# Scores from 64-wide queries and keys in TensorE's row halves, softmax on two batches at once

## What is computed

```python
q = jnp.einsum('bsd,hde->bhse', x, Wq)
k = jnp.einsum('bsd,hde->bhse', x, Wk)
v = jnp.einsum('bsd,hdf->bhsf', x, Wv)
s_a = jnp.einsum('bhie,bhje->bhij', k, q) / e
attn = jax.nn.softmax(s_a, axis=-1)
ax = jnp.einsum('bhtf,bhit->bhfi', v, attn)
...
out = a_flat @ Wlt
```

## Time and profile before

| | us |
|---|---|
| median of 3 runs | 1500.25 |
| lowest, highest | 1497.04, 1500.66 |
| the profiled execution | 1500.72 |
| its span, first to last instruction | 1498.9 |
| TensorE matmul busy | 1399.7 (93%) |
| VectorE busy | 1184.3 (79%) |
| ScalarE busy | 1008.2 (67%) |
| GpSimd (POOL) busy | 788.0 (53%) |
| mean granted TensorE clock | 0.979 |

### The profile page before, as it was taken

One profiled execution on the slowest core, in us unless ns is written; L12 is line 12 of the kernel. 1 busy time (PEld: TensorE's weight loads), 2 busy tenths in 40 slices (PEclk: granted clock), 3 DMA queues, 4 the chain that ended last, 5 costly groups with the idle time before them and its releaser, 6 DMA issues.

```text
span 1498.9 us, 32061 instructions
## 1 busy us (share of the span) xinstructions
PE 1399.7 (93%) x7812; PEld 1121.1 (75%) x7812; DVE 1184.3 (79%) x3231; ACT 1008.2 (67%) x2311; POOL 788.0 (53%) x888
## 2 busy tenths in 40 slices
PE   5899999999999999999998988898987999999993
PEld 4677888888888888888886766666765888888871
DVE  2988898989899898989897688777777766666655
ACT  2677887878887888878786666666654555555540
POOL 1675444444444444444442477767666565665561
PEclk8999999999999999999999999999999999999997
DMA  3422222222222222222224988777755787777779
GB/s 85 154 76 73 88 100 76 91 80 87 87 80 91 76 91 80 101 80 91 79 78 144 297 273 273 219 233 227 223 172 198 279 292 254 249 251 246 243 284 362
DMA packets 180725, 245.76 MB, mean 164 GB/s; under 512 B 32641, under 2 KB 143761, under 8 KB 180657
## 3 DMA queue, kind: packets, MB, share of 16 engines
q1 hardware_dynamic: 159872, 206.57, 41.5%
q0 software_dynamic: 13920, 31.33, 6.4%
q10 hardware_dynamic: 6864, 7.09, 1.4%
HBM read 99.85 MB, written 89.51 MB: 126 GB/s over the span
## 4 chain that ended last, share of the span: by engine, by line
PE 70%; DVE 11%; POOL 7%; issue 7%; DMA 2%; ACT 2%; SPq 1%; DVEq 0%; POOLq 0%; ACTq 0%
PE bank L403 15%; PE bank L405 13%; PE bank L404 13%; PE pair_ps L1690 10%; PE bank L1621 5%; PE bank L1715 5%; POOL sorted_scratch L839 5%; PE pair_ps L1854 1%; PE bank L1611 1%; POOL rstdB L833 1%; PE bank L1789 1%; DMA yearly<-y_scratch 1%; PE pair_ps L405 1%; PE pair_ps L403 1%; PE bank L1629 1%
## 5 line engine op out<-in xcount | busy, mean ns | idle before, releaser
L697 POOL TENSOR_TENSOR prob<-expo,inv 92x368 f32<-92x368 f32 x256 | 205.0, 801 | 394.6 <-DVE inv L1219 394.6
L874 POOL DMA_INDIRECT y_scratch<-ytok,tin x198 | 194.0, 980 | 124.1 <-issue 91.9
L839 POOL DMA_INDIRECT sorted_scratch<-trow,posi x184 | 180.2, 979 | 96.0 <-issue 57.5
L1690 PE MATMUL pair_ps<-z,xnT 128*92 128x368 f32 x512 | 201.3, 475 | 0.0
L1212 DVE TENSOR_REDUCE peak<-pair_ps 92x4 f32<-92x368 f32 x256 | 136.1, 532 | 73.2 <-PE pair_ps L1690 73.1
L1403 DVE SCALAR_TENSOR_TENSOR hid_l<-bank,hid_h 128x512 fp32r<-128x512 f32 (+1 forms) x159 | 103.5, 655 | 93.7 <-ACT hid_h L1040 92.7
L914 ACT ACTIVATE z<-bank 128x368 f32<-128x368 f32 x254 | 121.2, 477 | 63.0 <-PE bank L405 55.9
L953 ACT ACTIVATE w2s<-bank 128x368 fp32r<-128x368 f32 x256 | 122.5, 478 | 47.4 <-PE bank L405 43.0
L960 ACT ACTIVATE expo<-cent 92x368 f32<-92x368 f32 x256 | 130.4, 509 | 31.2 <-DVE cent L1224 28.2
L1040 ACT ACTIVATE hid_h<-bank 128x512 fp32r<-128x512 f32 (+1 forms) x159 | 90.5, 569 | 78.9 <-PE bank L405 78.3
L1239 DVE TENSOR_TENSOR w2s<-bank,w2s 128x368 fp32r<-128x368 f32 x256 | 136.2, 532 | 6.0 <-ACT w2s L953 3.1
(11 more groups left out here) (274 smaller groups left out, 3875.3 us busy)
## 6 DMA issues: line engine op xcount, KB each, us to landing
ax_scratch<-val SPq DMA_DIRECT2D x64, 736.0 KB, 3.8
arow<-ax_scratch SPq DMA_DIRECT2D x92, 512.0 KB
w1t<-w1s SPq DMA_DIRECT2D x53, 512.0 KB, 3.2
w2t<-w2s SPq DMA_DIRECT2D x53, 512.0 KB, 3.0
tin<-sorted_scratch SPq DMA_DIRECT2D x46, 260.0 KB
xin<-in_x_dram SPq DMA_DIRECT2D x32, 372.0 KB
ywide<-y_scratch SPq DMA_DIRECT2D x32, 256.0 KB, 7.2
h_scratch<-hP SPq DMA_DIRECT2D x32, 184.0 KB, 5.1
```

The lines of the kernel that those rows point to most:

```text
L697: nc.gpsimd.tensor_tensor(prob[:, k % 2], expo[:, k % 2], inv[:, k % 2].unsqueeze(2).to_broadcast([S, HH, S]), ALU.mult).then_inc(prob_kep ...
L839: pool.indirect_dma_start(out=sorted_dram, out_offset=bass.IndirectOffsetOnAxis(ap=posi[:, q, choice, r:r + 1], axis=0), in_=trow[:, q, ch ...
L874: pool.indirect_dma_start(out=y_dram, out_offset=bass.IndirectOffsetOnAxis(ap=tin[:, b, r, D:D + 1].bitcast(I32), axis=0), in_=ytok[:, b % ...
L1690: mm(score_ps[k % 2][0:S, 0:GT], xnT[:, q, b * S:(b + 1) * S], z[:, b, half * HH:(half + 1) * HH, :], start=True, stop=True).then_inc(scor ...
```

## The change

The products of `Wq` and `Wk` are no longer formed. The opening splits the weights themselves (`split_qk`) into `wqk_h` and `wqk_l`, eight slots of 128 columns: slot 2t holds the queries' weights of heads 2t and 2t + 1 side by side, slot 2t + 1 those of the keys. `project_qk` takes the place of `make_z`, with the same three matmuls, places and steps, and `qk[:, s]` of z: rows 0 to 63 of a slot belong to the even head, rows 64 to 127 to the odd one. The scores of two units (two batches, four heads) are made together at the head of every even step: eight float32 matmuls of 92 columns of weights, 64 rows and 92 columns, which go to rows 0 to 63 and 64 to 127 by turns, the lower rows to the one score bank and the upper ones to the other. `peak`, `cent`, exp, `total` and `inv` each treat both units in one instruction: `peak`, `cent` and exp in the even step, `total` and `inv` in the odd one. POOL's product, the transposes, the mix and the values stay per unit. `cent` and `expo` keep their size and are now one room for a pair of units instead of two rooms by turns. Heads within four are now in the order 0, 2, 1, 3 (`head_of`), which the value weights and the place in `val` follow. The copy `xnT` is gone.

```diff
+def head_of(n):
+    return n // HH * HH + n % 2 * 2 + n % HH // 2
...
+        score_ps = pair_ps[0:S].rearrange("i (u n) -> i u n", u=2)[:, :, 0:GT].rearrange("i u (k t j) -> i u k t j", k=2, t=2)
...
-        Z_FIRST = {6: 9, 7: 11}
-        Z_MID = {2: 5, 3: 7, 5: 8}
-        Z_THEN = {1: 4, 2: 6, 6: 10}
+        QK_FIRST = {6: 9, 7: 11}
+        QK_MID = {2: 5, 3: 7, 5: 8}
+        QK_THEN = {1: 4, 2: 6, 6: 10}
...
-                at_least(pool, inv_kept, n + 1)
-                at_least(pool, exp_kept, n + 1)
+                at_least(pool, inv_kept, UN // 2 * g + k // 2 + 1)
+                at_least(pool, exp_kept, UN // 2 * g + k // 2 + 1)
...
-                A(z[:, :, h, :], room[:, 0:GT].rearrange("d (b j) -> d b j", b=GB), ACT.Copy).then_inc(z_kept, 1)
+                A(qk[:, h], room[:, 0:GT], ACT.Copy).then_inc(qk_kept, 1)
...
-                if exists(g):
-                    n = UN * g + k
-                    at_least(act, cent_kept, n + 1)
-                    at_least(act, prob_kept, n - 1)
-                    A(expo[:, k % 2], cent[:, k % 2], ACT.Exp, scale=1.0 / E).then_inc(exp_kept, 1)
+                if exists(g) and k % 2 == 0:
+                    pair = UN // 2 * g + k // 2
+                    at_least(act, cent_kept, pair + 1)
+                    at_least(act, prob_kept, 2 * pair)
+                    A(expo[:], cent[:], ACT.Exp, scale=1.0 / E).then_inc(exp_kept, 1)
...
+            def split_qk(j):
+                src = raw[:, j * H * E:(j + 1) * H * E].rearrange("d (t n) -> d t n", n=2 * E)
+                dve.wait_ge(ws_qk, 32)
+                V.tensor_copy(wqk_h[:, j:H:2], src).then_inc(wqkh_kept, 1)
+                dve.wait_ge(wqkh_kept, j + 1)
+                V.tensor_tensor(wqk_l[:, j:H:2], src, wqk_h[:, j:H:2].bitcast(F32), ALU.subtract).then_inc(wqkl_kept, 1)
...
+                pair = UN // 2 * g + k // 2
+                if exists(g) and k % 2 == 0:
+                    if k == 2 and exists(g + 1):
+                        at_least(dve, sixes_kept, g + 2)
+                    at_least(dve, score_done, 2 * (pair + 1))
+                    V.tensor_reduce(peak[:], score_ps, AX_X, ALU.max).then_inc(peak_kept, 1)
                 if k == 2 and exists(g + 1):
                     keep_moments(g + 1)
+                if exists(g) and k % 2 == 0:
+                    at_least(dve, peak_kept, pair + 1)
+                    at_least(dve, exp_kept, pair)
+                    V.tensor_tensor(cent[:].rearrange("i k (u t) j -> i u k t j", u=2), score_ps,
+                                    peak[:].unsqueeze(4).to_broadcast([S, 2, 2, 2, S]), ALU.subtract).then_inc(cent_kept, 1)
+                if exists(g) and k % 2 == 1:
+                    at_least(dve, exp_kept, pair + 1)
+                    V.tensor_reduce(total[:], expo[:], AX_X, ALU.add).then_inc(total_kept, 1)
+                    at_least(dve, total_kept, pair + 1)
+                    at_least(dve, prob_kept, 2 * pair)
+                    V.reciprocal(inv[:], total[:]).then_inc(inv_kept, 1)
...
-                    at_least(pe, z_kept, H * g + (half + 1) * HH)
-                    at_least(pe, cent_kept, n - 1)
-                    mm(score_ps[k % 2][0:S, 0:GT], xnT[:, q, b * S:(b + 1) * S], z[:, b, half * HH:(half + 1) * HH, :],
-                       start=True, stop=True).then_inc(score_done, 1)
+                if exists(g) and k % 2 == 0:
+                    half = k // GB
+                    at_least(pe, qk_kept, H * g + (half + 1) * HH)
+                    at_least(pe, cent_kept, UN // 2 * g + k // 2)
+                    for n in range(4):
+                        nk, t = n // 2, n % 2
+                        at = slice((k + nk) % GB * S, ((k + nk) % GB + 1) * S)
+                        for u in (0, 1):
+                            queries, keys = (qk[u * E:(u + 1) * E, half * HH + 2 * t + side, at] for side in (0, 1))
+                            ins = mm(score_ps[:, u, nk, t], keys, queries, start=True, stop=True)
+                            if n == 3:
+                                ins.then_inc(score_done, 1)
```

More of the change, by code:

```diff
@@ L34 @@
 WARM = 4
-LAG_S, LAG_T, LAG_TK, LAG_M, LAG_V = 1, 2, 3, 4, 8
+LAG_T, LAG_TK, LAG_M, LAG_V = 2, 3, 4, 8
 CT = 512
@@ L203, in build @@
         tokb = sb("tokb", [D, 1], stack=first)
-        pair_h = sb("pair_h", [D, H, D], F32R, stack=first)
-        pair_l = sb("pair_l", [D, H, D], F32R, stack=first)
+        wqk_h = sb("wqk_h", [D, H, 2 * E], F32R, stack=first)
+        wqk_l = sb("wqk_l", [D, H, 2 * E], F32R, stack=first)
         wv_h = sb("wv_h", [D, H, D], F32R, stack=first)
@@ L217, in build @@
         xtok = sb("xtok", [S, GB, D], stack=first)
-        xnT = sb("xnT", [D, 2, GT], stack=first)
         xn_h = sb("xn_h", [D, GT], F32R, stack=first)
@@ L222, in build @@
         xtok_l = sb("xtok_l", [S, 2, GB, D], F32R, stack=first)
-        z = sb("z", [D, GB, H, S], stack=first)
-        peak = sb("peak", [S, 2, HH], stack=first)
+        qk = sb("qk", [2 * E, H, GT], stack=first)
+        peak = sb("peak", [S, 2, 2, 2], stack=first)
         cent = sb("cent", [S, 2, HH, S], stack=first)
@@ L341, in build @@
         cs = sem("cs")
-        qkT_done, qkT_kept, pair_done, pair_kept = (sem(n) for n in ("qkT_done", "qkT_kept", "pair_done", "pair_kept"))
+        wqkh_kept, wqkl_kept = (sem(n) for n in ("wqkh_kept", "wqkl_kept"))
         split_v, split_lt, high_kept, low_kept, split_c = (sem(n) for n in (
@@ L968, in step @@
                         at_least(act, val_out[half], 16 * gv)
-                    A(val[:, half, :, h % HH, :], val_ps[:, 0:GT].rearrange("f (b i) -> f b i", b=GB),
+                    A(val[:, half, :, head_of(h) % HH, :], val_ps[:, 0:GT].rearrange("f (b i) -> f b i", b=GB),
                       ACT.Copy).then_inc(val_kept, 1)
-                keep_zs(g, k, Z_THEN)
+                keep_qks(g, k, QK_THEN)
                 if k == 0 and exists(g + 1):
@@ L1636, in turn_xn, with project_qk @@
                 ins.then_inc(xn_done, 1)
-            def make_z(g, h, room=front_ps[1], opening=False):
+            def project_qk(g, h, room=front_ps[1], opening=False):
                 if not opening:
-                    at_least(pe, z_kept, H * g + h)
+                    at_least(pe, qk_kept, H * g + h)
                 if h == 0:
-                    at_least(pe, xnT_kept, g + 1)
+                    at_least(pe, xnh_kept, g + 1)
                     at_least(pe, xnl_kept, g + 1)
@@ L1645, in make_z, with project_qks @@
                         at_least(pe, xT_kept, KC * (g + 2))
-                three(room[:, 0:GT], pair_h[:, h], pair_l[:, h], xn_h[:], xn_l[:],
-                      True, True).then_inc(z_done, 1)
-            def make_zs(g, k, when):
+                three(room[:, 0:GT], wqk_h[:, h], wqk_l[:, h], xn_h[:], xn_l[:],
+                      True, True).then_inc(qk_done, 1)
+            def project_qks(g, k, when):
                 if k in when and exists(g + when[k] // H):
-                    make_z(g + when[k] // H, when[k] % H)
+                    project_qk(g + when[k] // H, when[k] % H)
             for c in range(KC):
@@ L1657, in _ @@
                 embed(0, piece)
-            pe.wait_ge(ws_qk, 32)
-            for j in range(4):
-                for m in range(4):
-                    o = (4 * j + m) * E
-                    ins = nc.tensor.transpose(bank[2 + j][0:E, m * D:(m + 1) * D], raw[:, o:o + E], ident[:])
-                ins.then_inc(qkT_done, 1)
-            turn_first(0)
-            pe.wait_ge(qkT_kept, 4)
-            for j in range(2):
-                for m in range(4):
-                    h = 4 * j + m
-                    qT = raw[0:E, 2048 + h * D:2048 + (h + 1) * D]
-                    kT = raw[0:E, 2048 + (H + h) * D:2048 + (H + h + 1) * D]
-                    ins = mm(bank[6 + j][:, m * D:(m + 1) * D], qT, kT, start=True, stop=True)
-                ins.then_inc(pair_done, 1)
+            turn_first(0)
             for c in range(KC):
```

92 lines of the change are left out of this document (26 added, 66 removed).

## The result

| | before | after |
|---|---|---|
| median, us | 1499.78 (4 runs) | 1565.71 (4 runs) |
| lowest, highest | 1497.04, 1500.66 | 1563.86, 1566.89 |
| profiled execution (span) | 1500.72 (1498.9) | 1565.93 (1564.0) |
| TensorE matmul busy | 1399.7 (93%) | 1403.5 (90%) |
| VectorE busy | 1184.3 (79%) | 1150.8 (74%) |

The ratio is 1.044, 95% interval 1.0424 to 1.046: slower by 66 us. The forecast was 1597 with a range from 1535 to 1660.

What follows compares the result with a forecast made beforehand. TensorE was taken as the bound. Per group, 19.27 us of other work + 3.5 of new waits + 4 x 1.15 for bursts = 27.4, against 24.23; 32 groups add 101 us, the opening -4: 1597 us, range 1535 to 1660.

Steps and rivals of the forecast that it cites:

- the sign: TensorE's busy share in 150 to 750 us was to fall below 93%, with idle time in odd steps.
- The new waits: TensorE waits in odd steps for VectorE and ScalarE behind the pair softmax: 3.5 us per group, 112 us in all.
- step 2: Steps 2 to 3 of a group: with moments and varA in the chain, TensorE was to wait 1.19 us.
- X: Price of one score burst on TensorE, four per group: 1.15 us taken, against 1.24 for two scores before.
- overlap with both changes of form: Burst price if the row halves run together and entering and leaving the 64-row form is paid: 1.02 us.
- the gap at 22.0 us: About 0.2 us between matmul starts after the opening's 64-row matmuls, where 0.12 is usual; 0.15 booked per change of form.
- the high end: Burst price if the halves do not overlap and both changes of form are paid: 1.58 us.
- The opening: Start of the kernel: without four copies, pair products and their splits in the chain, 4 us less.
- the first rival: Halves gain fully, waits as forecast: X 0.72 to 1.02, 25.7 to 26.9 us per group, 1542 to 1581 us; chance 0.20.
- Halves one after the other: Row halves in the burst do not run side by side: X 1.28 to 1.58, 1614 to 1652 us; chance 0.15.
- The costly alternation: Each alternation of halves in a burst costs like a change of form: X about 2.5, near 1770 us; chance 0.03.
- The hidden chain: Longer VectorE and ScalarE chain before the odd step stays hidden, no new waits: 1427 to 1465 us; chance 0.12.

Runs made afterwards that it cites:

- E9: Changed kernel with the pair burst kept, but maximum, centring, exp, sum and reciprocal per unit with the old lags: 1507.45 us, 1.0044 of the kernel before.
- E2: Kernel before with its full-height scores, both units' scores at the head of the even step and the softmax on two units at once: 1620.19 us, 1.0797.
- E11: E9 with probability transposes first in odd steps, and moments and varA of step 2 behind mix_l: 1472.19 us, 0.981 of the kernel before.
- E1: Changed kernel with all four matmuls of the lower rows first, then those of the upper rows: 1614.67 us, 1.076 of the kernel before.
- E3: Changed kernel with row halves kept, but scores of one unit in every step and the softmax of the kernel before: 1498.31 us, 0.9986.
- E6: Changed kernel, even steps: VectorE makes probT_l and mix_l between maximum and centring, ScalarE does exp last: 1571.74 us, 1.0475 of the kernel before.
- E10: E7 with ScalarE's exp also last in the even step: 1564.61 us, 1.0424 of the kernel before.
- E5: Changed kernel with ScalarE's exp last in even steps, behind the value and qk copies: 1562.82 us, 1.0416 of the kernel before.
- E7: Changed kernel with the burst issued in the odd step before, behind the probability transposes and ahead of the values: 1534.62 us, 1.0228 of the kernel before.
- E12: Changed kernel, pair softmax kept, with the same two moves as E11: 1529.09 us, 1.0188 of the kernel before.

## Why the prediction was right

**What bounds.** Right. TensorE's own work was the whole chain before, and the trace had no room for a later VectorE. From 150 to 750 us TensorE's busy share is 552.44 of 600, 92.1%, under the 93% that the prediction named as the sign.

**The new waits.** Right in mechanism, place and releaser. Forecast from burst to odd step were 2.95, 3.55, 2.95 and 3.65 us; measured 2.94, 3.15, 2.95 and 3.61. The pieces that gave them: `peak` 921 ns and `cent` 912 (taken as 940), exp 817 (880).

Only step 2 was off, by 0.4, and that is `varA`. The prediction took the 2.79 us of before from maximum to TensorE and made it longer. In that stretch `varA` began while POOL's product of the probabilities ran, and ended with it:

```profile
411.26 0.80 POOL L697 TENSOR_TENSOR prob<-expo,inv 92x368 f32<-92x368 f32 x1 [1.75 <-DVE inv L1219]
...
411.52 0.56 DVE L1156 TENSOR_SCALAR varA<-moments 92x4 f32<-92x4 f32 x1
```

The same instruction takes 557 ns in every group of 150 to 750 us before (555 in E9), and 154 ns in the changed kernel, where no product of POOL runs beside it. That is the 0.4 us. That POOL's product is what holds it is read from these times; no run tried it.

The transposes of hT began 3.70 us behind the burst, where 3.75 was forecast, and their weight load did stand still for hT, for 0.31 us. The chain does not show it as idle time. The mix in front of them took 408.54 - 407.78 = 0.76 us there, not 0.5, and the four transposes 0.64, not 0.44. The first projection of steps 4 and 5 likewise began at 3.69 us, with 3.65 forecast.

From burst to burst (6.57, 6.67, 6.74 and 6.61 us) less the same stretches before (6.14, 6.15, 5.83, 6.11), with 0.22 added for the faster scores, the new waits are 0.65, 0.74, 1.13 and 0.72 us, against 0.64, 1.09 (1.19 less the 0.1 that was there), 1.13 and 0.65. Counted from the mean group, 26.53 - 19.27 - 4 x 1.02 = 3.2 us of waits, against 3.5 in the sum. That it agrees so closely is in part luck. In the chain a matmul that was waited for takes 0.41 us instead of 0.17, which the prediction left out. Against that, the 0.11 us of slow start behind the burst lies inside the wait and was counted in X as well, and the wait of step 2 before was 0.35 us, not 0.1.

E2 bears the mechanism out with the halves taken away, E9 by taking the pair softmax away.

**X, the price of a burst.** The step that was mis-sized: *"I take X = 1.15 us, the middle of 0.72 and 1.58"*. In the change it is the 0.26 us from the last matmul's start to the burst's (403.64 to 403.90) less the usual 0.17, then 0.82 to the start of the mix (404.72), then 0.28 instead of 0.17 to its second matmul (405.00): 1.02 us; E11 gives 1.01. That is the end "overlap with both changes of form" of the prediction, not the middle: the halves overlap fully, in 0.65 us (0.72 there), and the changes of form cost 0.36 to 0.37 (0.30 booked from the gap at 22.0 us). That both add up to 1.02 is luck: the passes were booked 0.07 too high and the changes of form 0.07 too low. The reason I gave for leaning to the high end, that no row shows an overlap, was a lack of evidence and I used it as evidence against.

**The sum.** X too high by 0.13, four times, and waits too long by 0.3 make 0.8 us per group: 27.4 forecast, 26.53 measured. A group grew by 2.25 us instead of 3.15, which is 29 us of the 31 between 1597 and 1566. The opening gained 28.22 - 25.15 = 3.1 us to the first projection (booked 4). With both, the sum would be 1569. The last 3 us lie in the first part, which grew from first to last score by 66 us (773.8 to 840.2), not by 32 x 2.25 = 72: not every one of the 32 groups grew like those of the middle. Which do not was not looked at. From the last score to the end it took 691.3 us before and 692.4 after.

The case that came true is the first rival, full gain on the halves with the waits as above: its X ends at 1.02, its group at 26.9 and its time at 1581. It had a chance of 0.20, the forecast with X in the middle 0.50. The range holds 1566 because it took in both ends of X.

**The rivals.** Halves one after the other: E1 built it nearly, 1615 us, inside that rival's 1614 to 1652, and the change is 49 us better. The costly alternation: refuted by the burst of 0.87 us. The hidden chain: it takes less than 0.9 us of new waits per group; the change has 3.2. E11 shows that it was no idle rival: with the softmax per unit and the two moves, 1472 us.

**The rule weighed against the trace.** By the Trainium skill's page TensorEngine Tiling (Array Packing), Key Properties, different tiles work in parallel, and a change of tiling mode drains the engine. The runs agree with both: the halves worked in parallel (0.65 us for 16 passes instead of 1.28), and the change of form had a price (about 0.36 us in and out, by E3 and by E11's 1.01 - 0.65). By the first alone the prediction would have had 0.72. At one unit per burst the price of the change of form decides (E3: no gain). The span model of the Trainium skill's page TensorE: Matmul & The Clock Gate, Part 3, gave 0.64 us for the burst in the prediction. The trace agrees for the passes (0.65 us), while the burst as a whole cost 1.02. The pairs within it start 6 to 7 ns apart.

**Where the 66 us are.** By E9, 58 us are the pair softmax behind a burst; the other 8 are what the pair burst still costs with a softmax per unit. I read them as what is left of the covers lost (the odd step's score in front of its mix) after 0.23 x 4 x 32 = 29 us gained; the covers were not measured apart. E11's moves win 35 us back.

## What to carry to other kernels

Merging two evictions into one instruction of double width saves VectorE 0.14 us of busy time per pair (0.92 for 2 x 0.53). But both units must then be worked on in one step, and everything behind in that engine's order waits 1.79 us instead of one unit's 0.9 (an estimate, 2 x 0.45). Where the engines have little room, cost a merge by the chain from producer to next consumer. Look at what work covered that chain and whether the same change moves it away: here the burst took the odd step's score, and with it 0.62 us of cover. A faster step on the bounding engine should be tried with the softmax, or whatever follows, left as it was; then look for independent work (transposes, statistics) that can stand in front of the wait. A duration read from one place of a trace can hold a collision that the change removes, as `varA` with its 557 and 154 ns.

## What the runs showed that I had not expected

The two row halves pair their passes. In the timeline of the changed kernel, cut to 403.899 to 403.909 us:

```profile
403.90 0.16 PEld L1668 LDWEIGHTS pair_ps<-qk 64*92 64x92 f32 x2 [0.23 <-issue]
403.90 0.32 PE L1668 MATMUL pair_ps<-qk 64*92 64x92 f32 x2
```

Two passes are under way within those 10 ns, and so are two weight loads. The row does not name their halves, but the four transposes, passes of 92 columns over full height, stand 0.08 us apart, so I read them as one of each half, though the program issues both passes of the lower half's matmul first. All of them:

```profile
L1668 PE MATMUL pair_ps<-qk x16: 242/242/313, 403.9 to 404.6; 64*92 64x92 f32 x16
```

Sixteen passes start in 403.9 to 404.6, in eight pairs, 0.08 us apart but for the first gap of 0.15. That is 0.65 us, what eight passes of 92 columns take. In E1 the halves are 8 passes apart in the program and still overlap in part (1.23 us, not 1.50). The 16 weight loads start in pairs too, against the rival's point that every pass brings a weight load of its own.

The second surprise is E6 and E10: of two moves meant to shorten one wait each, the two together were 9 us worse than one alone (E6 against E5), or 30 us (E10 against E7). With both units' softmax in the even step no order that I tried came below 1529 us (E12). With the odd unit's back in the odd step it was 1507 and 1472 (E9, E11).
